# A transformer block on one core: turned branches in one block, an earlier check, and 20 and 36 unused transposes

## The reference

```python
q, k, v = split(x @ Wqkv)                       # Wqkv 512 x 1536
q = layernorm(q) * q_ln_scale; k = layernorm(k) * k_ln_scale
scores = where(causal, -inf, (q / sqrt(32)) @ k.T)      # per head
x = layernorm(x + (softmax(scores) @ v) @ out_W)
g = x @ ((gate_w - 128) * gate_scale).T         # gate_w, up_w 2048 x 512 int32
u = x @ ((up_w - 128) * up_scale).T
x = layernorm(x + (silu(g) * u) @ ((down_w - 128) * down_scale).T)
```

## Time and profile before

| | |
|---|---|
| runs | 2361.03, 2362.65, 2364.99 us |
| profiled execution | 2362.58 us, span 2360.8 us, granted TensorE clock 0.989 |
| TensorE matmul | 2304.4 us busy (98%) |
| VectorE | 1770.3 us busy (75%) |
| ScalarE | 1292.6 us busy (55%) |
| GpSimd | 248.5 us busy (11%) |
| projection | 0 to 326 us |
| attention | 326 to 1533 us |
| head of the last stage | 1533 to 1557 us |
| feed-forward | 1557 to 2361 us |

### The profile page before, as it was taken

One profiled execution on the slowest core, in us unless ns is written; L12 is line 12 of the kernel. 1 busy time (PEld: TensorE's weight loads), 2 busy tenths in 40 slices (PEclk: granted clock), 3 DMA queues, 4 the chain that ended last, 5 costly groups with the idle time before them and its releaser, 6 DMA issues. The chain is left out here.

```text
span 2360.8 us, 34413 instructions
## 1 busy us (share of the span) xinstructions
PE 2304.4 (98%) x12578; PEld 1417.2 (60%) x12578; DVE 1770.3 (75%) x1813; ACT 1292.6 (55%) x1633; POOL 248.5 (11%) x275
## 2 busy tenths in 40 slices
PE   8999979999999999999999999989999999999997
PEld 7888844444444444444444444378888888888886
DVE  7776748998889988899898998955556555565554
ACT  4444458888888888888888888711111111111121
POOL 2111111110021100211002110000000000000001
PEclk9999979999999999999999999989999999999999
DMA  7767784100921008210082101441111021110100
GB/s 252 260 243 256 241 248 94 37 20 6 185 51 33 24 6 170 60 33 24 6 163 68 33 24 41 143 156 36 36 36 54 19 72 36 37 54 18 36 19 18
DMA packets 126303, 197.51 MB, mean 84 GB/s; under 512 B 14488, under 2 KB 39576, under 8 KB 126112
## 3 DMA queue, kind: packets, MB, share of 16 engines
q1 hardware_dynamic: 126128, 195.25, 29.6%
HBM read 122.83 MB, written 72.37 MB: 83 GB/s over the span
## 5 line engine op out<-in xcount | busy, mean ns | idle before, releaser
L1045 ACT ACTIVATE probs<-score 128x1024 f32<-128x1024 f32 (+3 forms) x1152 | 1000.3, 970 | 177.0 <-PE score L957 175.0
L1108 DVE TENSOR_TENSOR total<-total,probs 128x2048 f32<-128x2048 f32 (+3 forms) x468 | 983.9, 2102 | 79.8 <-POOL probs L919 22.8
L957 PE MATMUL score<-queries,keys 98*128 98x512 f32 (+3 forms) x2304 | 641.9, 406 | 13.3 <-issue 6.4
L957 PEld LDWEIGHTS score<-queries,keys 98*128 98x128 f32 x2304 | 381.2, 189 | 435.3 <-ACT probs L1045 349.9
L1448 ACT ACTIVATE hidden<-slot,gate_scale_sb 128x512 f32<-128x512 f32 x128 | 88.2, 689 | 634.5 <-PE slot L1378 634.5
L973 PE MATMUL ctx_acc<-probs,values 128*32 128x512 f32 (+3 forms) x3584 | 421.9, 561 | 0.0
L1517 DVE SCALAR_TENSOR_TENSOR hidden<-slot,up_scale_sb,hidden 128x512 f32<-128x512 f32 x128 | 96.1, 751 | 255.2 <-ACT hidden L1448 250.3
L919 POOL TENSOR_SCALAR_AFFINE_SELECT probs<-probs 128x512 f32<-128x512 f32 x128 | 167.1, 1307 | 1010.7 <-ACT probs L1045 1010.7
L1378 PE MATMUL slot<-xt_hi,w_front 128*128 128x512 f32 x608 | 238.2, 392 | 1.5 <-DVE xt_lo L1558 1.5
L1378 PE MATMUL slot<-xt_lo,w_front 128*128 128x512 f32 x608 | 237.9, 391 | 0.0
L973 PEld LDWEIGHTS ctx_acc<-probs,values 128*32 128x32 f32 x3584 | 85.4, 108 | 194.0 <-issue 147.7
(11 more groups left out here) (135 smaller groups left out, 2188.5 us busy)
## 6 DMA issues: line engine op xcount, KB each, us to landing
keys<-k_hi SPq DMA_DIRECT2D x64, 256.0 KB
queries<-q_hi SPq DMA_DIRECT2D x64, 256.0 KB
wq_int<-in_wq SPq DMA_DIRECT2D x48, 256.0 KB, 3.2
wq_float<-wq_f SPq DMA_DIRECT2D x48, 256.0 KB, 2.9
x_raw<-in_x_t SPq DMA_DIRECT2D x32, 256.0 KB, 3.7
v_rows<-v_out SPq DMA_DIRECT2D x32, 256.0 KB, 2.3
q_hi<-part_hi SPq DMA_DIRECT2D x32, 256.0 KB, 2.6
q_lo<-part_lo SPq DMA_DIRECT2D x32, 256.0 KB, 3.1
```

The costliest lines, as they stand in the source:

```text
L957: ins = pe.matmul(score[u % RING][:, i, cut(t):], keys[0:ROWS, kb // ST, h, kb % ST * P:(kb % ST + 1) * P], queries[0:ROWS, q_buffer[ch], ...
L1045: act.activation(probs[:, t % PB, 2 * p:2 * p + 2, cut(t):], score[u % RING][:, :, cut(t):], ACT.Exp).then_inc(exped, 1)
L1108: dve.tensor_tensor(into, into, now, ALU.add).then_inc(added, 1)
```

## The change

It does these things together.

1. *Start of `project`.* TensorE does 20 transposes of the identity that nobody reads (`WARM`) before its first product. The first chunk's joint start takes four units instead of three.
2. *End of `project`.* The last chunk's first four own jobs (`spare`) put their parts into `x_hi` and `x_lo`, which are free by then, and don't wait for a store; the last four wait only for the stores of the chunk before. The maximum of the last weight tile and the check of all weights move ahead of the last two low parts on VectorE, and the norms' reductions come one unit earlier.
3. *Behind the check.* TensorE does 36 transposes of the identity (`STAY`) into the other `turn` bank, after the two of the check and ahead of the end of the block.
4. *Branches.* The flags are turned round (`is_le` for `is_gt`: 1 is the usual case). `attend` and `finish` are one block. Each engine reads `plain`, TensorE also `narrow`, and holds attention and the last stage in one `If` body, with a second copy of both for the general case in `Else`. So the usual code follows the branch, the second barrier and the second reading are gone, and at the very end each engine jumps over the `Else` body. TensorE's choice by `narrow` stays as a branch between attention and the head.
5. *The seam of attention and the head.* The casts of the head (`cp_hi`) are ScalarE's, which also copies the last sums; VectorE begins the head behind its last sum, and TensorE's last `sum_total` opens the head.
6. *The 11 steps* whose sum TensorE takes are spread to the ends of 11 equal stretches and no longer to their middles, so that the last step of a group is one of them.

```diff
+    WARM = 20
+    STAY = 36
...
+        def spare(own, i):
+            return own and i < DC
+        def parts(own, i):
+            return (x_hi[:, 0, i, :], x_lo[:, 0, i, :]) if spare(own, i) else (part_hi[:, i % 4, :], part_lo[:, i % 4, :])
...
-                    if before or u >= 3:
+                    if before or u >= ACCS:
...
-                            for m in range(3):
-                                pe.wait_ge(w_low_done, 3 * dc + m + 1)
-                                ins = product(acc[m], par, 0, m, dc)
+                            for a, (st, m) in enumerate(units[:ACCS]):
+                                pe.wait_ge(w_low_done, 3 * dc + (m if st == 0 else 2) + 1)
+                                ins = product(acc[a], par, st, m, dc)
...
             pe.wait_ge(ident_ready, 1)
+            for k in range(WARM):
+                pe.transpose(norms[k // DC % 2][:, k % DC * P:(k % DC + 1) * P], ident[:], ident[:])
...
             ins.then_inc(check_turned, 1)
+            for k in range(STAY):
+                pe.transpose(turn[1][:, k % DC * P:(k % DC + 1) * P], ident[:], ident[:])
...
-                act.wait_ge(parts_stored[i % 4], 64 * o + 32 * (i // 4) + 32)
+                if not spare(own, i):
+                    act.wait_ge(parts_stored[i % 4], 64 * o + 32 * (i // 4) + (0 if own else 32))
...
+                    if not after and u == NU - 1:
+                        widest(n, u // 2)
+                        dve.wait_ge(whole_done, 2 + WT * NCH)
+                        dve.tensor_reduce(check[:, 1:2], whole[:], AX.X, ALU.max).then_inc(fin, 1)
                     for own, i in jobs:
-                        low(n if own else c, i)
+                        low(own, n if own else c, i)
                         if i % DC == DC - 1:
-                            tops.append((n if own else c, i // DC, u + 3))
-                    if u % 2:
+                            tops.append((n if own else c, i // DC, u + (2 if own else 3)))
+                    if u % 2 and (after or u < NU - 1):
                         widest(n, u // 2)
...
-            dve.tensor_tensor(flag_f[:], check_top[:], limits[:], ALU.is_gt).then_inc(fin, 1)
+            dve.tensor_tensor(flag_f[:], check_top[:], limits[:], ALU.is_le).then_inc(fin, 1)
...
-    pe_sums = {late[(2 * i + 1) * len(late) // (2 * PE_SUMS)] for i in range(PE_SUMS)}
+    pe_sums = {late[(i + 1) * len(late) // PE_SUMS - 1] for i in range(PE_SUMS)}
...
-            sum_total(NG - 1, NCH - 1)
...
-            take_sums(NG - 1, NCH - 1)
...
+                last_total(pe)
+                pe.sem_inc(slot_free, FREE)
                 out(0)
                 out(1)
                 pe.wait_ge(ident_ready, 1)
                 for st in range(ST):
                     if st + 2 < ST:
+                        pe.wait_ge((ctx_taken, sums_taken)[st], NCH * NG + 1)
                         out(st + 2)
...
-            with pe.If(wide):
+            with pe.If(narrow):
+                program(lambda ap: ap)
+            with pe.Else():
                 program(lambda ap: ap.bitcast(F32))
-            with pe.Else():
-                program(lambda ap: ap)
...
+        def act_forward(act):
+            for st in range(ST):
+                h, rows = st // HALF, slice(st % HALF * P, (st % HALF + 1) * P)
+                act.wait_ge(head_scaled, st + 1)
+                act.activation(cp_hi[:, h, :, rows], y_raw[:, :, st * P:(st + 1) * P], ACT.Copy).then_inc(head_high, 1)
+            act.wait_ge(totaled, NCH * NG + 2)
+            act.wait_ge(keep["ctx_stored"][1], 32 * (NCH // 2) * NG)
+            act.activation(keep["sums_out"][:, 1, :], keep["sums_bank"][:], ACT.Copy).then_inc(sums_taken, 1)
...
+            head_scale(0)
+            for st in range(ST):
+                if st + 1 < ST:
+                    head_scale(st + 1)
+                head_low(st)
+            dve.wait_ge(totaled, NCH * NG + 2)
...
+        @block.tensor
+        def _(pe):
+            plain = pe.value_load(plain_flag, min_val=0, max_val=1)
+            narrow = pe.value_load(narrow_flag, min_val=0, max_val=1)
+            with pe.If(plain):
+                pe_attention(pe, False)
+                pe_forward(pe, narrow)
+            with pe.Else():
+                pe_attention(pe, True)
+                pe_forward(pe, narrow)
```

171 lines of the change are left out of this document (97 added, 74 removed).

## The result

The changed kernel took 2350.72 us, the median of five runs (2348.50 to 2353.37), against 2362.65 for the kernel before in the same session (2360.82 to 2366.50): ratio 0.995, 95% interval 0.9938 to 0.9962. The profiled execution took 2351.3 us with a span of 2349.4. All eleven have a median of 2352.2. The kernel before moved too, to 2361.09 in the second session, so the gain between medians of one session is 11.9 us in the first and 7.3 in the second; the forecast was 8.1. A large part of why one kernel gives both is what the experiments found.

A forecast was written before the change was run, and what follows sets the result against it. TensorE was taken to set the pace, busy 2304 of 2360.8 us, leaving 56 us idle to win. Terms -0.3 - 2.5 - 7.0 + 0 + 1.7 = -8.1 gave 2354.5 us, range 2350.0 to 2359.0.

The forecast's parts named there:

- The start, -0.3: Start of the projection: the fourth bank lets the unit reusing bank 0 begin at 20.56 instead of 20.82 us, about -0.3 us.
- The end of the projection: Projection's end, up to the flags: spare buffers (-2.8 us) and moved reductions (-1.8) bring the flags to 321.3 from 325.87.
- The transposes and the barrier, 5.8 us and 326.5: Behind the check: 36 transposes take 5.8 us, half at half clock, and the drain releases the barrier at about 326.5.
- rival A: At the barrier: the transposes don't hold it up; start of attention gains 5.7 us, total 2351.3 us; chance 0.18.
- Behind the barrier: Barrier to query loads: the usual case falls through without a jump, so queries are issued at 328.6 against 331.07 us.
- parts 2 to 4: From the projection's end through barrier and branch to the query loads: together -2.5 us, ends -0.6 and -5.7.
- rival B: At the branch: its time is the flag's late arrival, so two reads cost twice; 2362 us, no change; chance 0.05.
- The seam, -7.0: Attention to feed-forward: no barrier, branch falls through, residual add at 1536.0 instead of 1542.96; -7.0 us, ends -5.0 and -7.8.
- Attention, 0: TensorE's sum steps in attention: 11 per group as before, no work moved from the totals; 0, bound -1 and +2 us.
- The end, +1.7: Kernel end: SyncE jumps over the general program before waiting for the stores; +1.7 us, ends 0 and +2.1.
- Rival C: Start of each attention group: VectorE becomes the pace, 12.3 us in four groups; slower, 2366.8 us; chance 0.04.
- D: Long end jump and big block placement cost more: 3.7 us on each of three turns; 2365.5 us; chance 0.03.

The follow-up runs named there:

- e12: The changed kernel run again with nothing edited, in a later session; 2353.82 us, ratio 0.9963.
- e6: The changed kernel without the 20 transposes at the start and with three units in the joint start; 2351.13 us.
- e5: The changed kernel without the spare buffers: the last eight jobs' parts in the four old buffers, with their old waits; 2352.27 us.
- e4: The changed kernel with the general program as If body and the usual one as Else body, so the common case is reached by a jump; 2354.22 us.
- e2: The changed kernel with 72 transposes behind the check in place of 36; 2355.81 us.
- e1: The changed kernel without its 36 transposes behind the check; 2348.77 us.
- e3: The changed kernel with TensorE's 11 sum steps a group at their old places; 2354.70 us.
- e7: The changed kernel with SyncE's last four stores moved behind the end of the If; 2353.67 us.
- e10: The changed kernel without the 36 transposes, with the fourth chunk's queries loaded early and the last four stores behind the If; 2347.64 us.
- e8: The changed kernel without the 36 transposes and with the fourth chunk's queries loaded ahead of chunk 4's keys and values; 2346.71 us.
- e11: The changed kernel, 36 transposes kept, with the fourth chunk's queries loaded ahead of chunk 4's keys and values; 2350.80 us.
- e9: The kernel before the change, with only the fourth chunk's queries loaded ahead of chunk 4's keys and values; 2360.38 us, ratio 0.9991.

## Why the prediction was right where it was, and where not

The mechanisms of parts 2, 3, 4, 5 and 7 held; the sum came out 3.8 us too high against the first set and 0.7 too high against the second (2353.82). That the number is near is partly luck, for the terms miss in both directions. With the race for the fourth chunk's queries taken out, the spans are 8.3 us (first profile) and 9.1 us (e12) below before's, where the sum said 8.1. In that, the start of attention gave 1.2 and 1.4 us and not 2.8 (parts 1 to 4), and the seam with the moved sum steps 8.5 and 8.7 us and not 7.0. The race, which the forecast doesn't have, then gave 3.1 us in the first profile and took 2.3 in e12.

1. **The start, -0.3.** The fifth unit waits 1.8 us for VectorE's norm, as forecast, and starts at 20.29, 0.5 us earlier where 0.3 were worked out; in the variants with the new start it lies between 20.05 and 20.92 (before: 20.82). Nothing is left by 300 us (v store at 300.48, before at 300.39), and e6 shows no loss without it. The silent step, that an earlier start of the projection reaches its end, has nothing for it in the rows; a term of 0.3 us is below what these runs can tell.
2. **The end of the projection.** Forecast: last low part to 318.9, check at 319.9, flags written at 321.3. Measured: 319.3, 320.5, 321.9. The waits for the v stores are there, at 311.80 and 315.64 against 311 and 315.5. e5 gives 2.5 us to the buffers, against 2.8 forecast, which leaves 1.5 of the 4.0 for the moved reductions, against 1.8. That remainder wasn't tested by itself.
3. **The transposes and the barrier, 5.8 us and 326.5.** The drain does wait for them, so rival A's reason is refuted, although its number, 2351.3, is nearer to the first result than the forecast's; that nearness is luck. They took 6.8 us, since the clock came back about 1 us before their end and not half way; in six other executions 5.2 to 5.8, the forecast's size, and in one (e6) 6.75. The two slow ones and e4, whose jump follows, began attention at half clock; in the other five with 36, and in e2, the first six scores ran at 2.4 GHz. The part's lower end, 323.4 "since the stores need until then", was too low for the queries: in e1 they had to wait for a store until 325.6. The barrier was at 327.8, and at 326.1 to 327.7 in the others with 36 and the spare buffers.
4. **Behind the barrier.** 2.1 us to the first query load, as forecast (0.2 + 1.8 + 0.1). Queries at 329.89 and not 328.6, which is the late barrier: -1.2 for parts 2 to 4, not -2.5. The branch takes 3872 ns as a jump (e4) and 73 ns falling through, and rival B falls with that. The Trainium skill's 108 ns for a compare-and-branch (Advanced Engine Details and Errata, section Control Flow Timing), which the text went against, is near the second alone.
5. **The seam, -7.0.** From last sum to residual add 12.18 us became 5.26, -6.9, with VectorE's row of operations setting the end and the output product at full clock, step by step as forecast (eight operations in 5.3 us, 5.7 taken). The branch is 0.06 us in place of 4.1. Mis-sized is the 0.5 us for VectorE being free earlier: with the steps of part 6 it is 2.0, of which 1.1 lies behind chunk 2's copy and 0.9 ahead of it. From the residual add to feed-forward it takes 0.4 us more than before, which "follows as before" didn't have. e3 shows that a third of the gain (2.3 us) hangs on the last step's sum being TensorE's, which keeps its clock. The rest, the missing barrier, the branch and the casts on ScalarE, has its times in the rows, but no run takes one of them away alone.
6. **Attention, 0.** The step "no work is moved from the totals: 0" is wrong twice. The new places are worth 2.0 us within attention (e3), of which part 5 had counted 0.5. And the stretch is not carried through unchanged, since the forecast had put all of TensorE's idle time at the start, the two seams and the end. In the profile of before a wait of TensorE for queries, 2.18 us at 380.97, stood on the path. The earlier trace rows lists ScalarE's waits alone, and the forecast never asked for TensorE's. A shift of the start by 1.2 us was carried through one for one, when it is weighed against a queue of loads with its own pace. In the first profile the wait was gone (-3.1), in the second it was back and longer (chunks 0 to 2 +1.4).
7. **The end, +1.7.** +1.4 in the first profile, +1.6 in the second. From the last store's issue to SyncE's last wait it is 3.0 us, where 3.7 were taken for the jump. SyncE's own branch rows are 0.03 to 0.05 us long even where it jumps (2346.0 here); the time lies behind the row. e4 takes the term away by having no jump there, e7 hides it in the span but not in the time. The step that a span and a time are always the same distance apart held for the changed kernel to 0.2 us (1.9 to 2.0 against 1.8), and not for e7.

Rival C did not come: from 350 to 1531 us ScalarE waits for VectorE's sums four times, 2.1 us in all and at most 0.5, against three times and 1.6 us before. Nor did D in any part but the end: feed-forward takes 801.04 us against 801.29. TensorE has one long jump, 3.35 us from 2334.1, but its last matmul starts at 2335.81 and nothing of its own comes after it.

**What stays open.** Why the same loads take 2 to 3 us more in one execution than in another wasn't settled; the runs moved one load, and none varied their size or number. Whether a given execution has the wait is known for the profiled ones alone. Why e7 and e10 take 0.8 us and more outside the span is open as well. The same holds for the projection's end, whose flags lie between 321.6 (e7) and 325.7 (e2) in the profiles with the same code up to there.

**The better version.** e8 (ratio 0.9935, interval 0.9922 to 0.9949) and e10 (0.9941, interval 0.9927 to 0.9954) have lower ratios than the changed kernel in either of its sessions (0.995 and 0.9963). e8's interval lies clear of the second one's and overlaps the first's; e10's overlaps both. e1, which only leaves the transposes out, has 0.994 (0.9926 to 0.9953) and can't be told from them. What is shown best is that such transposes don't pay: in one session none and 72 of them, with nothing else changed, give 2348.77 us (2348.56 to 2349.65) and 2355.81 (2352.38 to 2357.23). For the 36 it is the gain over the kernel before, 14.9 us in e1 against 11.9 and 7.3, and the profiles of e1, e8, e10 and e11. The early queries are shown to help where the transposes stay (e11 against e12).

## What to carry to other kernels

Before an earlier start is carried through a stage one for one, look at the pace engine's own waits for transfers in that stage, and at how many microseconds they are away from appearing or going. Work that nobody reads, placed ahead of a barrier to hold the clock, moves the barrier by its whole duration, because the block's drain waits for it. Here what it kept of the clock was gone 2.6 us later in the first profile and reached the first six scores in others, worth 0.5 to 0.8 us against 5.2 to 6.8 spent. Let the common case follow the branch, and look in the execution's time, not only in the span, at what moving the remaining jump brings: e7's 1.1 us of span were hardly there in the time.

## What was not expected of the hardware

- A far jump goes with a burst of instruction loads, falling through almost without. These rows of the DMA section of the trace count them, for e4 from 327 to 333 us and then for the changed kernel from 328 to 334 us:

```profile
q14 instruction: 9, 0.07, 4.1%
q8 instruction: 2, 0.03, 2.7%
```

```profile
q14 instruction: 1, 0.01, 0.6%
```

  SyncE's first two query loads behind the jump took 1.9 to 2.3 us to issue (before, e4, e9) and 0.82 us in each of the other eleven profiles.
- The same transposes, at the same place, took 5.2 to 6.8 us by when the granted clock rose to 2.4 GHz.
- TensorE lost more than its wait each of the six times: from 1.68 us for queries and 2.6 lost (e3) to 3.11 us and 5.4 lost (e12). In the windows behind the wait its clock is at half. In e12, by the windows of the trace:

```profile
380.00:382.00 2.00, 2.00 (x5) 1.61 (x6) 1.90 (x2) 0.74 (x1) 0.00 (x0) 0.50 0.13 33
382.00:384.00 2.00, 2.00 (x8) 0.95 (x11) 0.77 (x1) 2.00 (x4) 0.64 (x1) 0.50 0.06 17
384.00:386.00 2.00, 2.00 (x10) 0.50 (x3) 0.88 (x1) 1.03 (x2) 0.00 (x0) 0.50 0.00 0
```
